# New hand-over lists for one turn of a fused attention kernel: the order of the steps on five engines and the table of PSUM banks

## The reference, cut to what matters

```python
scores = einsum('bhqd,bhkd->bhqk', q, k) / sqrt(dk)
sc = softmax(where(dam, scores, NEG)) * mask * dam
dist = sqrt(clip((sum(sc) - cumsum(sc)) * |i - j|, 0, None))
te = clip(exp(-softplus(gamma) * dist), 1e-5, 1e5)
scores = softmax(where(dam, where(mask, scores * te, NEG), NEG))
out = einsum('bhqk,bhkd->bhqd', scores, v)
x = layernorm(query + out @ oW.T + ob)
x = layernorm(x + relu(x @ w1.T + b1) @ w2.T + b2)   # layers 0 and 2
...
y = layer0(ctx); x = layer1(x); x = layer2(query=x, values=y)
out = layernorm(x + cross_attention(x, ctx) @ wo + bo)
```

## Time and profile before

| | us |
|---|---|
| median of three runs | 3225.2 (3223.77 to 3232.08) |
| the profiled execution | 3229.56 |
| span of that execution, first to last instruction | 3227.8 |
| TensorE busy | 2886.0 |
| VectorE busy | 2747.5 |
| ScalarE busy | 2698.7 |
| GpSimd busy | 772.5 |

### The profile page before, as it was taken

The page is one execution under the profiler, slowest core; times in us unless marked ns, Lnnn a source line. Parts: engine busy times, 40 slices in busy tenths (PEclk is TensorE's granted clock), DMA queues, the critical chain, the costliest instruction groups (busy, mean ns, idle before and its releaser), DMA issues.

```text
span 3227.8 us, 77600 instructions
## 1 busy us (share of the span) xinstructions
PE 2886.0 (89%) x21912; PEld 2151.5 (67%) x21912; DVE 2747.5 (85%) x5898; ACT 2698.7 (84%) x10212; POOL 772.5 (24%) x1116
## 2 busy tenths in 40 slices
PE   4699999999999999999999999999999999999996
PEld 3466666676676676676676667676667676676664
DVE  4788998888998888998888998888998888998883
ACT  3688988888888888888888888888888888898883
POOL 1122222222222222222222221222221222221220
PEclk7899999999999999999999999999999999999998
DMA  5010011010011010011010011010011010011000
GB/s 173 24 32 19 25 33 33 28 34 20 22 33 34 28 34 25 17 33 34 28 34 28 14 33 34 28 34 28 14 33 34 28 34 28 15 33 34 28 18 11
DMA packets 167467, 101.11 MB, mean 31 GB/s; under 512 B 37312, under 2 KB 166908, under 8 KB 167420
## 3 DMA queue, kind: packets, MB, share of 16 engines
q1 hardware_dynamic: 158668, 90.83, 10.2%
q10 hardware_dynamic: 8752, 9.71, 0.9%
HBM read 56.84 MB, written 10.01 MB: 21 GB/s over the span
## 4 chain that ended last, share of the span: by engine, by line
PE 41%; DVE 34%; ACT 13%; issue 8%; SPq 1%; DMA 1%; POOL 1%; DVEq 0%; ACTq 0%; POOLq 0%
PE gen_ps L645 15%; PE gen_ps L794 7%; DVE X L999 6%; ACT E L858 6%; PE scores_ps L691 4%; DVE E L990 4%; PE gen_ps L742 4%; DVE res L1040 4%; DVE X L1009 4%; PE gen_ps L701 3%; ACT X L858 3%; DVE res L1053 3%; DVE nm L1015 3%; PE gen_ps L653 2%; PE gen_ps L752 2%
## 5 line engine op out<-in xcount | busy, mean ns | idle before, releaser
L858 ACT ACTIVATE X<-X,nm 128x128 f32<-128x128 f32 x1536 | 595.8, 403 | 33.2 <-DVE nm L1015 32.6
L858 ACT ACTIVATE E<-scores_ps,nm 128x128 f32<-128x128 f32 x1536 | 541.7, 390 | 53.8 <-DVE nm L982 53.7
L645 PE MATMUL gen_ps<-f_buf,up_w 128*128 128x256 f32 x2048 | 479.9, 385 | 4.7 <-DVE f_buf L471 0.8
L794 PE MATMUL gen_ps<-down_w,hidden 128*128 128x256 f32 x2048 | 453.0, 379 | 1.3 <-ACT hidden L500 1.2
L982 DVE TENSOR_REDUCE nm<-scores_ps 128x8 f32<-128x1024 f32 x320 | 390.4, 1220 | 71.0 <-PE scores_ps L691 70.1
L1136 POOL TENSOR_SCALAR_AFFINE_SELECT X<-X 128x1024 f32<-128x1024 f32 x192 | 209.8, 1093 | 1003.0 <-DVE X L1009 1003.0
L645 PEld LDWEIGHTS gen_ps<-f_buf,up_w 128*128 128x128 f32 x2048 | 378.6, 190 | 86.2 <-DVE hidden L498 23.9
L990 DVE TENSOR_TENSOR_SCAN E<-chain,E 128x1024 f32<-128x1024 bf16 x192 | 430.1, 2240 | 0.0
L999 DVE SCALAR_TENSOR_TENSOR X<-E,rz,decay 128x128 f32<-128x128 f32 x1536 | 426.7, 349 | 2.2 <-DVE E L990 0.5
L701 PE MATMUL gen_ps<-ident,X 128*128 128x128 f32 x2560 | 382.5, 283 | 42.9 <-ACT X L858 20.3
L794 PEld LDWEIGHTS gen_ps<-down_w,hidden 128*128 128x128 f32 x2048 | 384.1, 190 | 51.7 <-issue 1.6
(11 more groups left out here) (143 smaller groups left out, 5215.2 us busy)
## 6 DMA issues: line engine op xcount, KB each, us to landing
k_diag<-k_f SPq DMA_DIRECT2D x768, 32.0 KB, 1.9
xk_diag<-xk_f SPq DMA_DIRECT2D x1024, 8.0 KB, 1.7
ctx_f<-in_ctxT SPq DMA_DIRECT2D x32, 256.0 KB, 2.7
x_f<-in_xT SPq DMA_DIRECT2D x32, 256.0 KB, 2.6
ctx_t<-in_ctx SPq DMA_DIRECT2D x32, 256.0 KB, 2.7
x_t<-in_x SPq DMA_DIRECT2D x32, 256.0 KB, 3.2
cx_f<-in_ctxT SPq DMA_DIRECT2D x32, 256.0 KB, 2.7
out<-out_t SPq DMA_DIRECT2D x32, 256.0 KB, 2.2
```

What stands on the lines that cost most here:

```text
L645: mm = nc.tensor.matmul(ps[:, i * T:(i + 1) * T], w[:, k, c * P:(c + 1) * P], src[:, k, :], start=(k == 0), stop=(k == C - 1))
L794: mm = nc.tensor.matmul(out, hidden[:, f, b * S:(b + 1) * S], down_w[l][:, f, :], start=(f == 0), stop=(f == FC - 1))
L858: a = nc.scalar.activation(dst[:, cols], src[:, cols], ACT.Exp, bias=minus_max[:, h:h + 1], accum_out=sums[:, h:h + 1])
```

## The change

All steps stay; the five lists give them another order, some another pair (d), and BANKS another bank. Fifteen read-outs of PSUM change their engine. To ScalarE go pt (3, 1, 1) half 1, pt (2, 0) half 1, pt (1, 1) half 0, v 0, up (2, 1), up (0, 1) and q; to VectorE go pt (3, 0, 0) half 1, pt (2, 0) half 0, both halves of pt (1, 0), v 2, turn (2, 1), up (2, 0) and up (0, 3). The deepest d stays 2. Nothing else of the program is touched. The diff, cut to the lists that are spoken of below; SYNC of before and parts of SCALAR are left out:

```diff
-TENSOR = [(1, ("scores", (2, 1))), (1, ("up", 0, 3)), (0, ("k", 0)), (1, ("up", 0, 0)), (2, ("att", (3, 0, 0))),
-    (2, ("pt", (3, 1, 1), 0)), (2, ("pt", (3, 1, 1), 1)), (1, ("down", 0)), (1, ("kx",)), (2, ("pt", (3, 1, 0), 0)),
-    (0, ("scores", (0, 0))), (2, ("pt", (3, 1, 0), 1)), (2, ("att", (3, 1, 1))), (1, ("pt", (2, 0), 0)),
-    (0, ("scores", (0, 1))), (2, ("att", (3, 1, 0))), (1, ("turn", 0, 2)), (1, ("pt", (2, 0), 1)), (1, ("v", 2)),
-    (1, ("pt", (2, 1), 0)), (1, ("pt", (2, 1), 1)), (1, ("att", (2, 0))), (0, ("k", 1)), (1, ("att", (2, 1))),
-    (1, ("o", 2)), (0, ("v", 1)), (0, ("v", 0)), (2, ("o", 3)), (0, ("scores", (1, 0))), (1, ("turn", 2, 1)),
-    (0, ("scores", (1, 1))), (0, ("pt", (0, 0), 0)), (1, ("up", 2, 0)), (1, ("up", 2, 3)), (1, ("up", 2, 2)),
-    (1, ("up", 2, 1)), (0, ("pt", (0, 0), 1)), (0, ("pt", (0, 1), 0)), (0, ("pt", (0, 1), 1)), (1, ("down", 2)),
-    (0, ("att", (0, 0))), (0, ("att", (0, 1))), (1, ("turn", 2, 2)), (1, ("q",)), (0, ("o", 0)),
-    (0, ("pt", (1, 0), 0)), (0, ("pt", (1, 0), 1)), (1, ("scores", (3, 0, 1))), (0, ("pt", (1, 1), 0)),
-    (0, ("pt", (1, 1), 1)), (0, ("att", (1, 0))), (0, ("att", (1, 1))), (1, ("scores", (3, 0, 0))), (0, ("o", 1)),
-    (1, ("vx",)), (1, ("scores", (3, 1, 0))), (1, ("pt", (3, 0, 1), 0)), (0, ("turn", 1, 1)),
-    (1, ("pt", (3, 0, 0), 0)), (1, ("pt", (3, 0, 1), 1)), (0, ("k", 2)), (1, ("pt", (3, 0, 0), 1)),
-    (1, ("scores", (3, 1, 1))), (0, ("turn", 0, 1)), (1, ("att", (3, 0, 1))), (0, ("up", 0, 1)),
-    (0, ("scores", (2, 0))), (0, ("up", 0, 2))]
...
-VECTOR = [(1, ("max2", (2, 0))), (1, ("sums", 0, 2)), (1, ("scores2", (2, 1))), (0, ("max1", (0, 0))),
-    (1, ("recip", (2, 0))), (1, ("kx",)), (1, ("tok", 0, 2)), (1, ("max2", (2, 1))), (1, ("turn", 0, 2)),
-    (2, ("att", (3, 1, 1))), (0, ("max1", (0, 1))), (1, ("pt", (2, 0), 1)), (0, ("dist", (0, 0))),
-    (1, ("recip", (2, 1))), (2, ("att", (3, 1, 0))), (0, ("x", (0, 0))), (0, ("dist", (0, 1))), (1, ("att", (2, 0))),
-    (1, ("att", (2, 1))), (0, ("x", (0, 1))), (0, ("scores2", (0, 0))), (1, ("sums", 2, 1)), (0, ("max2", (0, 0))),
-    (1, ("tok", 2, 1)), (0, ("scores2", (0, 1))), (0, ("max1", (1, 0))), (0, ("v", 0)), (2, ("sums", 3, 1)),
-    (0, ("max2", (0, 1))), (0, ("max1", (1, 1))), (1, ("up", 2, 3)), (0, ("dist", (1, 0))), (1, ("up", 2, 1)),
-    (0, ("x", (1, 0))), (0, ("recip", (0, 0))), (0, ("dist", (1, 1))), (0, ("recip", (0, 1))), (0, ("x", (1, 1))),
-    (0, ("scores2", (1, 0))), (1, ("sums", 2, 2)), (0, ("max2", (1, 0))), (1, ("tok", 2, 2)), (0, ("att", (0, 0))),
-    (0, ("scores2", (1, 1))), (0, ("att", (0, 1))), (0, ("max2", (1, 1))), (2, ("tok", 3, 1)), (1, ("q",)),
-    (0, ("recip", (1, 0))), (0, ("sums", 0, 1)), (0, ("recip", (1, 1))), (0, ("pt", (1, 1), 0)),
-    (1, ("max1", (3, 0, 1))), (0, ("att", (1, 0))), (0, ("att", (1, 1))), (1, ("max1", (3, 0, 0))),
-    (0, ("sums", 1, 1)), (0, ("tok", 1, 1)), (1, ("max1", (3, 1, 0))), (0, ("tok", 0, 1)), (0, ("k", 2)),
-    (1, ("recip", (3, 0, 1))), (1, ("pt", (3, 0, 1), 1)), (0, ("turn", 0, 1)), (1, ("max1", (3, 1, 1))),
-    (1, ("recip", (3, 0, 0))), (0, ("up", 0, 1)), (0, ("max1", (2, 0))), (1, ("att", (3, 0, 1))),
-    (1, ("recip", (3, 1, 0))), (0, ("up", 0, 2)), (0, ("max1", (2, 1))), (0, ("dist", (2, 0))),
-    (1, ("recip", (3, 1, 1))), (0, ("x", (2, 0))), (0, ("dist", (2, 1))), (0, ("x", (2, 1))),
-    (0, ("scores2", (2, 0))), (1, ("att", (3, 0, 0))), (1, ("pt", (3, 1, 1), 1))]
...
-POOL = [(1, ("select", (2, 1))), (1, ("widen", (2, 0))), (1, ("widen", (2, 1))), (0, ("select", (0, 0))),
-    (1, ("dev", 2, 1)), (0, ("select", (0, 1))), (0, ("widen", (0, 0))), (0, ("select", (1, 0))),
-    (0, ("widen", (0, 1))), (1, ("dev", 2, 2)), (2, ("dev", 3, 1)), (0, ("select", (1, 1))), (0, ("widen", (1, 0))),
-    (0, ("widen", (1, 1))), (0, ("dev", 0, 1)), (0, ("dev", 1, 1)), (1, ("widen", (3, 0, 1))),
-    (1, ("widen", (3, 0, 0))), (0, ("select", (2, 0))), (0, ("dev", 0, 2)), (1, ("widen", (3, 1, 1))),
-    (1, ("widen", (3, 1, 0)))]
...
+TENSOR = [(1, ("up", 0, 0)), (1, ("scores", (2, 1))), (1, ("up", 0, 1)), (2, ("att", (3, 0, 1))), (0, ("k", 0)),
+    (2, ("att", (3, 0, 0))), (2, ("pt", (3, 1, 1), 0)), (1, ("down", 0)), (2, ("pt", (3, 1, 1), 1)),
+    (2, ("pt", (3, 1, 0), 0)), (2, ("pt", (3, 1, 0), 1)), (2, ("att", (3, 1, 1))), (2, ("att", (3, 1, 0))),
+    (0, ("scores", (0, 0))), (1, ("turn", 0, 2)), (0, ("scores", (0, 1))), (1, ("kx",)), (1, ("pt", (2, 0), 0)),
+    (1, ("pt", (2, 0), 1)), (1, ("v", 2)), (1, ("pt", (2, 1), 0)), (1, ("pt", (2, 1), 1)), (1, ("att", (2, 0))),
+    (0, ("k", 1)), (1, ("att", (2, 1))), (1, ("o", 2)), (0, ("v", 0)), (0, ("v", 1)), (2, ("o", 3)),
+    (0, ("scores", (1, 0))), (1, ("turn", 2, 1)), (0, ("scores", (1, 1))), (0, ("pt", (0, 0), 0)), (1, ("up", 2, 1)),
+    (1, ("up", 2, 2)), (1, ("up", 2, 3)), (1, ("up", 2, 0)), (0, ("pt", (0, 0), 1)), (0, ("pt", (0, 1), 0)),
+    (0, ("pt", (0, 1), 1)), (1, ("down", 2)), (0, ("att", (0, 1))), (0, ("att", (0, 0))), (0, ("o", 0)),
+    (1, ("turn", 2, 2)), (0, ("pt", (1, 0), 0)), (0, ("pt", (1, 0), 1)), (1, ("q",)), (0, ("att", (1, 0))),
+    (0, ("pt", (1, 1), 0)), (0, ("pt", (1, 1), 1)), (1, ("scores", (3, 0, 1))), (0, ("att", (1, 1))),
+    (1, ("scores", (3, 0, 0))), (0, ("o", 1)), (0, ("turn", 0, 1)), (1, ("vx",)), (1, ("pt", (3, 0, 1), 0)),
+    (1, ("scores", (3, 1, 0))), (1, ("pt", (3, 0, 0), 0)), (0, ("turn", 1, 1)), (1, ("pt", (3, 0, 1), 1)),
+    (1, ("pt", (3, 0, 0), 1)), (0, ("k", 2)), (1, ("scores", (3, 1, 1))), (0, ("up", 0, 2)), (0, ("up", 0, 3)),
+    (0, ("scores", (2, 0)))]
+SCALAR = [(0, ("k", 0)), (1, ("ln", (2, 1))), (1, ("root", (2, 1))), (2, ("pt", (3, 1, 1), 1)),
+    (2, ("pt", (3, 1, 0), 0)), (2, ("pt", (3, 1, 0), 1)), (1, ("effect", (2, 1))), (2, ("spread", (3, 1, 1))),
+    (2, ("spread", (3, 1, 0))), (1, ("exp2", (2, 0))), (0, ("exp1", (0, 0))), (1, ("exp2", (2, 1))),
+    (1, ("pt", (2, 0), 1)), (0, ("exp1", (0, 1))), (1, ("pt", (2, 1), 0)), (1, ("pt", (2, 1), 1)),
+    (1, ("spread", (2, 0))), (0, ("ln", (0, 0))), (1, ("spread", (2, 1))), (0, ("root", (0, 0))),
+    (0, ("effect", (0, 0))), (0, ("k", 1)), (0, ("ln", (0, 1))), (0, ("root", (0, 1))), (0, ("v", 0)),
+    (0, ("effect", (0, 1))), (0, ("v", 1)), (0, ("exp2", (0, 0))), (0, ("exp1", (1, 0))), (1, ("up", 2, 1)),
+    (0, ("exp2", (0, 1))), (0, ("pt", (0, 0), 0)), (1, ("up", 2, 2)), (0, ("exp1", (1, 1))), (0, ("pt", (0, 1), 1)),
+    (0, ("ln", (1, 0))), (0, ("root", (1, 0))), (0, ("pt", (0, 1), 0)), (0, ("effect", (1, 0))),
+    (0, ("pt", (0, 0), 1)), (0, ("ln", (1, 1))), (0, ("spread", (0, 1))), (0, ("root", (1, 1))),
+    (0, ("spread", (0, 0))), (0, ("effect", (1, 1))), (0, ("exp2", (1, 0))), (1, ("turn", 2, 2)),
+    (0, ("exp2", (1, 1))), (1, ("q",)), (0, ("pt", (1, 1), 0)), (0, ("pt", (1, 1), 1)), (0, ("spread", (1, 0))),
...
+VECTOR = [(1, ("scores2", (2, 0))), (2, ("recip", (3, 1, 0))), (1, ("sums", 0, 2)), (1, ("max2", (2, 0))),
+    (1, ("tok", 0, 2)), (1, ("scores2", (2, 1))), (0, ("max1", (0, 0))), (1, ("turn", 0, 2)), (1, ("max2", (2, 1))),
+    (1, ("recip", (2, 0))), (2, ("att", (3, 1, 1))), (0, ("max1", (0, 1))), (2, ("att", (3, 1, 0))), (1, ("kx",)),
+    (1, ("pt", (2, 0), 0)), (0, ("dist", (0, 0))), (1, ("recip", (2, 1))), (1, ("v", 2)), (0, ("x", (0, 0))),
+    (0, ("dist", (0, 1))), (1, ("att", (2, 0))), (1, ("att", (2, 1))), (0, ("x", (0, 1))), (0, ("scores2", (0, 0))),
+    (1, ("sums", 2, 1)), (0, ("max2", (0, 0))), (1, ("tok", 2, 1)), (0, ("scores2", (0, 1))), (0, ("max1", (1, 0))),
+    (1, ("turn", 2, 1)), (0, ("max2", (0, 1))), (2, ("sums", 3, 1)), (0, ("max1", (1, 1))), (0, ("dist", (1, 0))),
+    (1, ("up", 2, 3)), (1, ("up", 2, 0)), (0, ("x", (1, 0))), (0, ("dist", (1, 1))), (0, ("recip", (0, 1))),
+    (0, ("recip", (0, 0))), (0, ("x", (1, 1))), (0, ("scores2", (1, 0))), (1, ("sums", 2, 2)), (0, ("att", (0, 1))),
+    (0, ("att", (0, 0))), (0, ("max2", (1, 0))), (0, ("scores2", (1, 1))), (1, ("tok", 2, 2)), (0, ("max2", (1, 1))),
+    (2, ("tok", 3, 1)), (0, ("recip", (1, 0))), (0, ("pt", (1, 0), 0)), (0, ("pt", (1, 0), 1)), (0, ("sums", 0, 1)),
+    (0, ("recip", (1, 1))), (0, ("att", (1, 0))), (1, ("max1", (3, 0, 1))), (0, ("att", (1, 1))), (0, ("tok", 0, 1)),
+    (1, ("max1", (3, 0, 0))), (0, ("sums", 1, 1)), (0, ("turn", 0, 1)), (0, ("tok", 1, 1)), (1, ("max1", (3, 1, 0))),
+    (1, ("recip", (3, 0, 1))), (1, ("pt", (3, 0, 1), 1)), (0, ("k", 2)), (1, ("max1", (3, 1, 1))), (0, ("up", 0, 2)),
+    (0, ("up", 0, 3)), (1, ("recip", (3, 0, 0))), (0, ("max1", (2, 0))), (1, ("pt", (3, 0, 0), 1)),
+    (1, ("recip", (3, 1, 1))), (0, ("max1", (2, 1))), (0, ("dist", (2, 0))), (1, ("att", (3, 0, 1))),
+    (0, ("x", (2, 0))), (0, ("dist", (2, 1))), (0, ("x", (2, 1))), (1, ("att", (3, 0, 0)))]
+POOL = [(1, ("dev", 1, 1)), (2, ("widen", (3, 0, 1))), (2, ("widen", (3, 0, 0))), (1, ("select", (2, 0))),
+    (2, ("widen", (3, 1, 1))), (2, ("widen", (3, 1, 0))), (1, ("dev", 0, 2)), (1, ("select", (2, 1))),
```

(11 more changed lines are left out.)

14 lines of the change are left out of this document (1 added, 13 removed), and 15 rows, old and new, of the table SCALAR.

## The result

The changed kernel takes 3154.6 us (median of three runs, 3153.5 to 3154.8) where the kernel before took 3225.2: a ratio of 0.978, 95% interval 0.977 to 0.979. The prediction was 3160. The profiled execution has a span of 3151.7 us; that of before, 3227.8, came from an execution 4 us longer than the median.

The account below looks back on a forecast made before the run. No engine is full; waits between engines bound the kernel. Five pieces sum to 93.3 us, 93.5 with hops; clock down in half the turns (96.1) gives 94.8, less 1.9 x 31: about 3165, put at 3160; range 3115 to 3222.

Parts of the forecast that it names:

- S1: Piece of a turn from sums (0, 2) to sums (2, 1), bound by VectorE: 21.3 us to become 22.6.
- S2: Piece from sums (2, 1) to tok (2, 2), bound by VectorE: 27.2 us to become 29.1.
- S5: Piece from down 0 to the next turn's sums (0, 2): stays 7.1 us.
- S3: Piece from tok (2, 2) to o 1, work hopping between engines, where the gain lies: 13.9 us to about 9.8.
- S4: Piece from o 1 to down 0, bound by TensorE: 26.4 us to become 24.7.
- likeliest case: TensorE's clock falls in about half of the turns: 94.8 us a turn, about 3160 in all; chance 0.45.
- The shared port: VectorE and GpSimd overlapping: widenings beside X products of (1, 1) cost VectorE 0.14 us twice, within the 0.2 bound.
- (c): Rival: VectorE stands behind GpSimd before tok (2, 2) for 1.5 us more; turn 96.3, 3212 us; chance 0.04.
- (a): Rival: TensorE's clock stays up in nearly every turn; turn 93.5, 3126 us; chance 0.2.
- (b): Rival: TensorE's clock falls in every turn as now; turn 96.1, 3207 us, or 95.4, 3184; chance 0.12.
- (e): Rival, slower: the clock stays down from q to beyond o 1, twice as long; turn 97.8, 3259 us; chance 0.12.
- (d): Rival: the loop's branch on TensorE is uncovered, 1.99 us; turn 96.8, 3228 us, no change; chance 0.07.

Follow-up runs that it names:

- e11: Kernel after plus filler transposes on TensorE: 4 ahead of att (0, 0), 12 ahead of turn (2, 2), 5 ahead of q; 3154.2 us, 0.978 of before.
- e6: Kernel before with only vx's PSUM bank changed, from 1 to 2; 3210.8 us, 0.995 of before.
- e10: Kernel after with vx moved to the wait in front of o 0, in PSUM bank 0, its ScalarE read-out ahead of exp2 (1, 0); 3155.8 us, 0.980 of before.
- e1: Kernel before plus filler transposes on TensorE: 12 ahead of att (0, 1), 7 ahead of turn (2, 2), 5 ahead of q; 3195.8 us, 0.991 of before.
- e7: Kernel after with TensorE's list cut behind turn (2, 2), so the loop's branch stands there, order unchanged; 3174.8 us, 0.983 of before.
- e5: Kernel before with o 0 ahead of turn (2, 2) and q on TensorE, and VectorE's matching steps reordered; 3310.6 us, 1.025 of before.
- e9: e5 with widen (0, 1) ahead of select (1, 0) on GpSimd and exp2 (1, 0) ahead of turn (2, 2) on ScalarE; 3250.0 us, 1.009 of before.

## Why the prediction came out right, point by point

**The sum.** Forecast with the clock up, 93.5; measured 94.15. S1 22.6 against 22.32, S2 29.1 against 28.93, S5 as said. S3 9.8 against 10.83, S4 24.7 against 24.99. The likeliest case was 94.8, a mean of turns with the clock up and down; the turns are all alike and 0.65 shorter. That 3160 lies within 6 us of 3154.6 is in part luck. Two errors of the turn stand against each other, 0.65 left out of the sum and 1.3 put in for a clock that costs nothing. And the turns were laid on wrongly: by the prediction's own rule, 3225.2 less 31 times what the turn loses against 96.72, the measured 94.15 would give 3146. The 9 us are the 4 by which the profiled execution was longer than the median, 2 from 96.72 for a mean turn of 96.66, 2 more in filling and draining, and 1 by which the profiled execution of after was shorter than its median.

**S3, the largest error.** It was 1.0 too short. Counted from the start of tok (2, 2), the parts of the chain that the sum named ran like this in the kernel after (the selection ends at 1515.36, the exponentials at 1519.95, ScalarE's copies at 1521.87):

| | forecast, about | measured |
|---|---|---|
| selection of (1, 1) done | 1.3 | 1.43 |
| its exponentials done | 5.7 | 6.02 |
| ScalarE's copies done | 7.6 | 7.94 |
| att (1, 1) starts | 7.7 | 8.69 |
| o 1 starts | 9.8 | 10.83 |

So 0.3 was lost by the end of the copies, and 0.65 in front of att (1, 1), for which the sum had no wait:

```profile
1521.37 1.03 PE L690 MATMUL scores_ps<-xk_diag,q_f 64*64 64x512 f32 x8
1522.62 0.44 PE L711 MATMUL gen_ps<-ident,rz_wide 128*128 128x128 f32 x2 [0.23 <-POOL rz_wide L1149]
```

TensorE is in scores (3, 0, 1) until 1522.40 and then waits 0.23 for the widening of (1, 1), which the prediction had named itself as what o 1 might wait for. The widening follows recip (1, 1), which stands behind sums (0, 1) on VectorE and starts at 1521.16, 1.2 behind the last exponential. So what ends last before o 1 is not the softmax of (1, 1) alone, as the sum had it: it is scores (3, 0, 1) on TensorE and sums (0, 1) on VectorE, within 0.2 of each other.

tok (2, 2) is a second thing that was wrong, and it cost less than it looks: 1.70 where I had kept the 0.87 of the earlier trace rows. Its two instructions as one group (shortest, median and longest in ns, first and last start), and the selection beside them in the timeline of GpSimd:

```profile
L1066 DVE SCALAR_TENSOR_TENSOR x_tok<-res,rstd,norm_b x2: 476/891/1306, 1513.9 to 1514.3; 128x256 f32<-128x256 f32 x2
```

```profile
1514.24 1.12 POOL L1135 TENSOR_SCALAR_AFFINE_SELECT X<-X 128x1024 f32<-128x1024 f32 x1 [2.57 <-DVE X L1008]
```

The second instruction, begun at 1514.3, ends at 1515.63, 0.27 behind the selection's 1515.36. The 0.83 are hardly paid. q could start 0.54 later for nothing (e11), and max2 (1, 1), which stands behind tok (2, 2), starts at 1515.56, 0.2 behind the selection that it needs in any case. The step that failed is in "The shared port": I looked for the overlap only between the widenings and the X products. That part was right (2.32 once, had 2.32 and 2.18), and rival (c), 1.5 us in S2, didn't come; but scores2 (1, 1) moved in front of tok (2, 2), and what scores2 releases is the selection. The Trainium skill, "SBUF — State Buffer", Who interferes with whom, says of a VectorE operation with two inputs in SBUF and a GpSimd operation that reads SBUF that they contend, and that the second to start blocks until the first is done; the 1306 ns beside a selection that began first agree, though not to the end: after a full wait the instruction's 0.48 would end 0.48 behind the selection and not 0.27. I had weighed that rule on the wrong pair.

**S4.** The size was right (26.4 - 1.4) and one term wrong. I took 0.85 off for vx's wait and called S4 TensorE's. It is two parts. From o 1 to k 2 a chain through VectorE sets the time, and TensorE's work beside it is cover (e6: 0.2 for 0.85; e10: 0 for 1.9). From k 2 to down 0 TensorE works without a stop: 18.40 before (1569.20 to 1587.60), 17.24 after. There the gain lies. Half 1 of the transposes of (3, 0, 0), turn (0, 1) and half 1 of those of (3, 1, 1) left that part, 0.5 each, the first two into the cover and the third behind down 0; of their 1.5 the 1.16 is left. I had counted only the third. The start of turn (0, 1), which I named as what fills a wait, is worth its 0.5 for being out of the second part.

**The clock.** Forecast: 1.9 a turn for a fall, 2.6 with the long ones, in half of the turns. Measured in the kernel before, a short fall cost 1.0 to 1.3 and the mean of short and long 1.8 to 2.0 (e1), so the term for one fall was too large and that it fits the mean is chance. The case for "half" was weak as well: the stretch of the earlier trace rows that was said to have no fall behind it, 103.40 to 110.20, runs into 4.29 us without work for TensorE (108.54 to 112.83), and from 112.20 to 114.20 the granted clock is 0.52. In the kernel after the clock still falls, in 9 of 27 turns looked at, but costs nothing (e11, and e10, where it doesn't fall), since it falls on o 0, and TensorE waits for tok (2, 2) behind it anyway. One such turn (columns as in e1):

```profile
2074.00:2076.00 2.00, 1.01 (x18) 0.58 (x18) 1.94 (x8) 1.67 (x4) 1.51 (x3) 1.00 0.00 0
2076.00:2078.00 2.00, 1.29 (x3) 1.11 (x4) 2.00 (x4) 1.15 (x3) 0.57 (x1) 0.63 0.00 0
2078.00:2080.00 2.00, 2.00 (x6) 1.44 (x6) 2.00 (x3) 2.00 (x11) 0.86 (x1) 0.52 0.00 0
2080.00:2082.00 2.00, 1.91 (x16) 1.46 (x14) 2.00 (x4) 1.72 (x8) 1.27 (x3) 1.00 0.00 0
```

So the clock costs nothing, as in rival (a), though not the way that I had put: it doesn't stay up in every turn, but its fall lies on work with slack. (a)'s 93.5 a turn and 3126 didn't come, because of what the sum lacked in S3. Rivals (b) and (e) didn't come. e7 shows how near (b) was: one gap of 0.20 us and the fall lies on q.

**The branch.** I took 0 to 0.3. In its new place it shows nothing, and 0.20 behind four transposes (e7). Rival (d), 1.99, is refuted for both places. The Trainium skill, "Runtime: NRT & Kernel Launch", Instruction fetch mechanics, has a taken branch stall when its target isn't in the fetched window; here no more than those 0.20 can be put down to it, and whether the target was in it no run shows.

**Where the 2.5 a turn come from.** Against the full-clock turn of before (e1, 94.88 with the smaller values of the table), S1 has +1.04, S2 +1.72, S3 -2.04, S4 -1.42: -0.70. The other 1.8 is the clock. With the 0.24 that the fillers of e1 may have cost it is -0.46 and 2.0. "S3 is where the gain lies" was right (14.65 to 10.83), but the prediction put it down to the chain alone; seven to eight tenths of the turn's gain are TensorE's work in S3 at full clock. The move of o 0 alone is no gain: it cost 2.5% in e5 and, with GpSimd's and ScalarE's order, still 0.9% in e9. What it still lacked there is, by the waits, the transposes ahead of q and q's read-out on ScalarE; neither was tried alone.

## What to carry to other kernels

Judge a stretch by the chain between its ends and not by the engine that looks full: work beside a chain is cover, and taking it away gains nothing (1.9 us moved, 0 gained), while work behind the chain counts in full. A step that moves in one engine's list takes with it the lists of the others, the banks and the DMA queue; ask for each what it waits for and what it releases, and what the released step collides with. If TensorE's clock falls in a stretch with waits, see first on which work the fall lies: in front of a wait it is free, on the critical matmuls it cost 1.8 to 2.0 us of 96.7. Fillers that keep the clock up are work too. One that is written to a bank which must be read out first holds up the step behind it (0.6 here), so look in the trace for what they cost before their run is read.

## What the runs showed of the hardware that was not expected

The place of the clock's fall is unstable. It moved from S3 into S1 and S2 when S3 was filled (e1), its long form was absent from one execution when 0.2 us had left S4 (e6), and it went from o 0 to q for a gap of 0.20 us (e7). A turn's length thus changes by 1 to 1.5 us for edits that have no such price of their own. What decides the place was not found.

A single VectorE instruction of 0.48 us was stretched to 1.31 beside a GpSimd selection of 1.12, while eight X products beside the widenings lost 0.14 together. What makes the two cases different was not tried.
